# Attention maxima by 64 queries with two heads in a bank's partition halves, and scores by halves of 64 keys

## What is computed

```python
# 16 heads of 8; S = 512; causal
q_cos, q_sin, k_cos, k_sin = ...            # layer 0; layer 1 has plain q and k
scores = (einsum('bhqd,bhkd->bhqk', q_cos, k_cos) + einsum('bhqd,bhkd->bhqk', q_sin, k_sin)) / sqrt(8)
scores = where(tril(ones((S, S))), scores, -inf)
attn = softmax(scores, axis=-1)
out = einsum('bhqk,bhkd->bhqd', attn, v)    # then @ Wo.T, added to x
```

## Time and profile before

| | |
|---|---|
| median of 3 runs | 1248.75 us (1247.88 to 1258.58) |
| the profiled execution | 1242.17 us, span 1240.6 us |
| busy in the span | PE 982.9 us (79%), PE weight loads 648.0, DVE 831.4 (67%), ACT 678.7 (55%), POOL 639.1 (52%) |
| attention 0 | about 390 to 640 us of the span |
| attention 1 | about 970 to 1240 us |

### The profile page before, as it was taken

The page is one execution under the profiler, slowest core; times in us unless marked ns, Lnnn a source line. Parts: engine busy times, 40 slices in busy tenths (PEclk is TensorE's granted clock), DMA queues, the critical chain, the costliest instruction groups (busy, mean ns, idle before and its releaser), DMA issues. The chain is left out here.

```text
span 1240.6 us, 25928 instructions
## 1 busy us (share of the span) xinstructions
PE 982.9 (79%) x8908; PEld 648.0 (52%) x8908; DVE 831.4 (67%) x1829; ACT 678.7 (55%) x1293; POOL 639.1 (52%) x908
## 2 busy tenths in 40 slices
PE   2789663999883999999985563399999599999997
PEld 1456431777671455555543342388888345555553
DVE  1566341799995899999945776033333699999992
ACT  1356443777730677777763644122222277777775
POOL 3467637468774345455440666211110367777774
PEclk9899866899996799999997665699999599999999
DMA  4422032577796222222200333466664112112211
GB/s 134 114 50 54 27 115 72 140 208 211 212 155 126 68 71 71 70 77 77 74 8 26 101 107 109 133 191 189 183 194 145 43 47 54 54 53 54 56 47 29
DMA packets 151525, 122.57 MB, mean 99 GB/s; under 512 B 31712, under 2 KB 134032, under 8 KB 151408
## 3 DMA queue, kind: packets, MB, share of 16 engines
q1 hardware_dynamic: 141664, 102.89, 30.4%
q0 software_dynamic: 8016, 17.71, 4.8%
q10 hardware_dynamic: 1728, 0.46, 0.2%
HBM read 75.75 MB, written 42.61 MB: 95 GB/s over the span
## 5 line engine op out<-in xcount | busy, mean ns | idle before, releaser
L2117 ACT ACTIVATE attend_probs<-attend_attend_ps 128x512 f32<-128x512 f32 x640 | 350.8, 601 | 155.0 <-PE attend_attend_ps L2185 146.9
L2084 POOL TENSOR_SCALAR_AFFINE_SELECT attend_probs<-attend_probs 128x512 f32<-128x512 f32 x256 | 159.7, 636 | 189.8 <-ACT attend_probs L2117 189.3
L2185 PE MATMUL attend_attend_ps<-attend_q,attend_ks 50*128 50x512 f16 (+3 forms) x1024 | 235.2, 306 | 22.4 <-ACT attend_probs L2117 19.9
L2153 PE MATMUL attend_attend_ps<-attend_ks,attend_q 48*128 48x512 f16 (+3 forms) x1024 | 191.7, 317 | 32.4 <-DMA attend_ks<-k_stack 24.8
L2198 PE MATMUL attend_attend_ps<-attend_probs,attend_vals 128*32 128x512 f32 (+3 forms) x2048 | 182.3, 453 | 0.0
L2280 DVE TENSOR_REDUCE attend_neg_max<-attend_attend_ps 128x2 f32<-128x1024 f32 x128 | 155.0, 1211 | 10.0 <-PE attend_attend_ps L2165 10.0
L2165 PE MATMUL attend_attend_ps<-identb,stairs 64*128 64x128 bf16 (+1 forms) x1280 | 144.6, 213 | 0.0
L2185 PEld LDWEIGHTS attend_attend_ps<-attend_q,attend_ks 50*128 50x128 f16 x1024 | 71.3, 94 | 118.2 <-ACT attend_probs L2117 76.9
L2282 DVE TENSOR_REDUCE attend_neg_max<-attend_attend_ps 128x2 f32<-128x768 f32 x128 | 121.7, 951 | 9.7 <-PE attend_attend_ps L2165 8.2
L2165 PEld LDWEIGHTS attend_attend_ps<-identb,stairs 64*128 64x128 bf16 x1280 | 104.5, 100 | 18.1 <-issue 4.9
L1900 PE MATMUL experts_experts_ps<-experts_rowsT,experts_w_in 128*128 128x256 f32 (+1 forms) x468 | 110.8, 387 | 1.6 <-ACT experts_rowsT L1849 1.5
(11 more groups left out here) (317 smaller groups left out, 1988.3 us busy)
## 6 DMA issues: line engine op xcount, KB each, us to landing
experts_w_in<-in_L_ffn_w_dram SPq DMA_DIRECT2D x78, 176.0 KB, 2.4
q_stack<-middle_parts SPq DMA_DIRECT2D x24, 256.0 KB
k_stack<-middle_parts SPq DMA_DIRECT2D x24, 256.0 KB
attend_q<-q_stack SPq DMA_DIRECT2D x64, 96.0 KB
attend_ks<-k_stack SPq DMA_DIRECT2D x64, 96.0 KB
middle_w_in<-in_L_ffn_W_dram SPq DMA_DIRECT2D x23, 256.0 KB, 2.6
middle_w_out<-in_L_ffn_W_dram SPq DMA_DIRECT2D x23, 256.0 KB, 3.0
experts_rows<-sorted POOLq DMA_DIRECT2D x39, 128.0 KB, 2.5
```

Of the source, the lines that this page charges most:

```text
L2084: pool.affine_select(out=block_, in_=block_, compare_op=ALU.is_ge, fill=0.0, base=0, pattern=[[0, GH], [1, P]], channel_multiplier=-1).the ...
L2117: act.activation(probs[:, u.par, 2 * c + side, :], ps[:, PROB + side, :], ACT.Exp, scale=SCALE ** -2)\
L2153: pe.matmul(ps[:, bank + side, col:col + (qt + 1) * P], q[rows(side, KR), g, pair, qt * P:(qt + 1) * P], ks[rows(side, KR), g, pair, 0:(qt ...
L2185: mm = pe.matmul(ps[:, PROB + side, col:col + S - kt * P], ks[rows(side, KM), g, pair, kt * P:(kt + 1) * P], q[rows(side, KM), g, pair, kt ...
```

## The change

Maxima are taken by blocks of 64 queries (QS = 8 of them). In each of PE's products for the maxima the output is 64 partitions x up to 512 columns, and two heads share a bank, one in partitions 0 to 63 and one in 64 to 127; pair 0 and pair 1 have a bank each and opposite halves (`half`), so the four heads use the four quarters of the array. Chunks are now one or two blocks (`max_chunk`): 8 | 7 and 1 | 6 and 2 | 5 and 3 | 4 times 64 keys. The stairs are one matmul for each head and chunk, over both blocks. DVE reduces with one instruction for each block. The maxima of a unit lie by pair, part and block in the 32 partitions of `maxT` and by head in its columns, so four DMAs, each from 16 partitions x 64 columns, take them to `q`. The probabilities' products are cut in halves of 64 keys (outputs of 64 partitions), with the same banks, columns and order. ACT's, POOL's and the mix's work is as before.

```diff
+    H, QS = P // 2, 2 * QT
...
-        neg_max = sb("neg_max", [P, 2, 2, HP, QT])
-        max_parts = sb("max_parts", [P, 2, 2, 2, HP * QT], F16)
-        maxT = sb("maxT", [2 * GH * QT, 2, P], F16)
+        neg_max = sb("neg_max", [P, 2, HP, QS])
+        max_parts = sb("max_parts", [P, 2, HP, 2, QS], F16)
+        maxT = sb("maxT", [HP * 2 * QS, 2, P], F16)
...
-        max_in = [signal(f"max_in{i}", 2, 16) for i in range(2)]
+        max_in = [signal(f"max_in{i}", GH, 16) for i in range(2)]
...
         def max_chunk(c):
-            if c == 4:
-                return [(0, 1, 0), (1, 1, 256)]
-            return [(c // 2, 3, 0)] if c % 2 == 0 else [(c // 2, 2, 0), (c // 2, 0, 384)]
+            if c == 0:
+                return [(QS - 1, 0)]
+            return [(QS - 1 - c, 0), (c - 1, (QS - c) * H)] if c < 4 else [(3, 0)]
+
+        def half(side, pair):
+            first = H * ((side + pair) % 2)
+            return slice(first, first + H)
...
-                    for side in range(2):
-                        sp.dma_start(q[64 * side + KR:64 * side + KM, u.group, :, :], maxT[16 * side:16 * side + 16, u.par, :])\
-                          .then_inc(max_in[u.par].sem, 16)
+                    for pair in range(HP):
+                        for side in range(2):
+                            sp.dma_start(q[64 * side + KR:64 * side + KM, u.group, pair, :],
+                                         maxT[pair * 2 * QS:(pair + 1) * 2 * QS, u.par, half(side, pair)]).then_inc(max_in[u.par].sem, 16)
...
-                for n, (pair, qt, col) in enumerate(blocks):
-                    for side in range(2):
-                        pe.matmul(ps[:, bank + side, col:col + (qt + 1) * P], q[rows(side, KR), g, pair, qt * P:(qt + 1) * P],
-                                  ks[rows(side, KR), g, pair, 0:(qt + 1) * P], start=(n == 0), stop=False)
...
+                for n, (qs, col) in enumerate(blocks):
+                    for pair in range(HP):
+                        for side in range(2):
+                            pe.matmul(ps[half(side, pair), bank + pair, col:col + (qs + 1) * H],
+                                      q[rows(side, KR), g, pair, qs * H:(qs + 1) * H], ks[rows(side, KR), g, pair, 0:(qs + 1) * H],
+                                      start=(n == 0), stop=False)
+                diagonal = [col // H + qs for qs, col in blocks]
+                apart = diagonal[-1] - diagonal[0] if len(blocks) == 2 else 1
+                for pair in range(HP):
+                    for side in range(2):
+                        here = slice(64 * side, 64 * side + 64)
+                        span = ps[half(side, pair), bank + pair, :].rearrange("p (n t) -> p n t", t=H)
+                        mm = pe.matmul(span[:, diagonal[0]:diagonal[-1] + 1:apart, :], k.stairs[here, H + H * side:P + H * side],
+                                       k.identb[here, here].unsqueeze(1).broadcast_to([64, len(blocks), H]), start=False, stop=True)
+                    mm.then_inc(scored.sem, 1)
...
                 for pair, kt, col in prob_chunk(c):
-                    mm = pe.matmul(ps[:, PROB + side, col:col + S - kt * P], ks[rows(side, KM), g, pair, kt * P:(kt + 1) * P],
-                                   q[rows(side, KM), g, pair, kt * P:S], start=True, stop=True)
+                    for first in (0, H):
+                        mm = pe.matmul(ps[first:first + H, PROB + side, col:col + S - kt * P],
+                                       ks[rows(side, KM), g, pair, kt * P + first:kt * P + first + H], q[rows(side, KM), g, pair, kt * P:S],
+                                       start=True, stop=True)
...
+                for qs, col in max_chunk(c):
+                    ins = dve.tensor_reduce(neg_max[:, u.par, :, qs], pair_banks[:, :, col:col + (qs + 1) * H], X_AXIS, ALU.max, negate=True)
```

More of the change, by code:

```diff
@@ L2150, in maxima @@
                 blocks = max_chunk(c)
-                for n, (pair, qt, col) in enumerate(blocks):
-                    for side in range(2):
-                        pe.matmul(ps[:, bank + side, col:col + (qt + 1) * P], q[rows(side, KR), g, pair, qt * P:(qt + 1) * P],
-                                  ks[rows(side, KR), g, pair, 0:(qt + 1) * P], start=(n == 0), stop=False)
-                first = blocks[0][2] + blocks[0][1] * P
-                apart = blocks[1][2] + blocks[1][1] * P - first if len(blocks) == 2 else P
@@ L2158, in maxima @@
-                start = first // apart * apart
-                for half in range(2):
-                    for side in range(2):
-                        stair = P // 2 + P // 2 * side - P // 2 * half
-                        here = slice(64 * side, 64 * side + 64)
-                        span = ps[:, bank + side, start:start + apart * len(blocks)].rearrange("p (n t) -> p n t", t=apart)
-                        col = first - start + 64 * half
-                        mm = pe.matmul(span[:, :, col:col + 64], k.stairs[here, stair:stair + P],
-                                       k.identb[here, here].unsqueeze(1).broadcast_to([64, len(blocks), 64]),
-                                       start=False, stop=(half == 1))
-                        if half == 1:
-                            mm.then_inc(scored.sem, 1)
+                for n, (qs, col) in enumerate(blocks):
[4 more added lines that the diff above has]
+                                      start=(n == 0), stop=False)
@@ L2171, in turn_maxima @@
             def turn_maxima(u):
                 pe.wait_ge(parts_done.sem, parts_done.done(u))
-                pe.matmul(ps[0:2 * GH * QT, TURN, 0:P], max_parts[:, u.par, :, :, :].rearrange("p s a b -> p (s a b)"),
+                pe.matmul(ps[0:HP * 2 * QS, TURN, 0:P], max_parts[:, u.par, :, :, :].rearrange("p h a s -> p (h a s)"),
                           k.identh[:, :], start=True, stop=True)\
@@ L2179, in probabilities @@
                 if c == 0 and side == 0:
-                    pe.wait_ge(max_in[u.par].sem, (u.pair + 1) * 32)
+                    pe.wait_ge(max_in[u.par].sem, max_in[u.par].done(u.pair))
                 if u.past(1) or c >= 1:
@@ L2274, in reduce @@
                 pair_banks = ps[:, first:first + 2, :]
[L2275 to L2283 removed]
+                for qs, col in max_chunk(c):
+                    ins = dve.tensor_reduce(neg_max[:, u.par, :, qs], pair_banks[:, :, col:col + (qs + 1) * H], X_AXIS, ALU.max, negate=True)
                 ins.then_inc(maxed.sem, 1)
             def split_maxima(u):
[L2288 removed]
+                flat = neg_max[:, u.par, :, :]
                 parts = max_parts[:, u.par, :, :, :]
@@ L2300, in copy_maxima @@
                 if u.past(2):
-                    dve.wait_ge(max_in[u.par].sem, u.pair * 32)
-                dve.tensor_copy(maxT[:, u.par, :], ps[0:2 * GH * QT, TURN, 0:P])\
+                    dve.wait_ge(max_in[u.par].sem, max_in[u.par].done(u.pair - 1))
+                dve.tensor_copy(maxT[:, u.par, :], ps[0:HP * 2 * QS, TURN, 0:P])\
                    .then_inc(maxT_ready.sem, 1)
```

10 lines of the change are left out of this document (removed).

## The result

| | before | after |
|---|---|---|
| median | 1249.18 us (4 runs) | 1297.0 us (1285.65 to 1309.69, 4 runs) |
| profiled execution | 1242.17 us, span 1240.6 | 1289.64 us, span 1288.1 |
| attention 0, first to last CAST | 232.8 us | 244.6 us |
| attention 1, first to last CAST | 234.8 us | 264.5 us |

The ratio is 1.0336, 95% interval 1.022 to 1.0452: slower by some 3.4%. It leaves out the longest of the four executions after, 1309.69 us, which counts as a slow run (clock 0.87); the median takes in all four. (CAST is the copy of the turned maxima, L2302 before, L2306 after; its start is C. There are 32 in each attention.

The account below looks back on a forecast made before the run. DVE bounds the kernel, the maxima's way back 0.56 us behind; four issues make plain steps 7.96 us. Four steps gain +1.8 and +1.45, times 7.5, plus 5 for ends, less 2: +27 us, 1276 us, range 1228 to 1306.

Parts of the forecast that it names:

- the likeliest case: Whole kernel: four DMA issues delay PE's scores, plain step 7.96 against 7.23 us; 1276 us, by itself 1263 to 1290; chance 0.62.
- Rival E: PE, idle 2.1 us in each 8, loses its clock in some steps: +24 us, 1300 us; chance 0.04.
- What bounds the kernel: Plain step of 7.23 us: DVE runs almost without a hole; the maxima's way back has 0.56 us of slack.
- Four issues, 0.64 us apart: SP's queue behind each CAST: four maxima DMAs instead of two, 0.64 us from start to start, the last starting at C+2.22.
- Rival B: SP's four issues cost no more than two, so DVE's gain shows: plain step 6.68 us, 1217 us; chance 0.12.
- D: Gain and loss meet, with a DMA issue near 0.4 us: 1244 to 1260 us; chance 0.12.
- PE gets its maxima at C+2.22+2.21: PE's first scores: 2.21 us after the last issue starts at C+2.22, so C+4.43 instead of C+3.15.
- Row end 8.03: Step holding the end of a batch row: PE's shorter chunks 3 and 4 bring it to 8.03 us against 8.21.
- Reductions, -0.6 us: DVE's maxima reductions: 4608 elements in 8 instructions instead of 5120 in 7; DVE needs about 6.5 us a step.
- Quarters run all at once: PE's maxima matmuls: four array quarters overlap, about -0.3 us a step; wrong if chunk c=2 takes over 0.8 us to its mix.
- Gotcha 2 and the load price: PE weight loads: column tiling excludes the fast load; 84 loads 4.5 us, PE some 8.1 us if none hidden.
- Attention 1, "+1.45" for four steps: Attention 1: four steps, 30.45 us before, grow by 1.45 us, against +1.8 in attention 0.

Follow-up runs that it names:

- x9: The kernel after with attention 1's gathers left out except for the first 128 rows, which are joined to every row: 1262.22 us, ratio 1.0127.
- x1: The kernel before with four maxima DMAs instead of two, and none of the 64-row parts: 1263.04 us, ratio 1.0185.
- x4: The kernel after with two maxima DMAs instead of four, the maxima turned with three matmuls: 1243.05 us, ratio 1.0008.
- x6: The kernel after with the second of attention 1's two gathers a unit, and its join, left out: 1278.84 us, ratio 1.0226.
- x8: x4 with DVE's subtraction that forms the low parts moved behind the c=0 reduction: 1272.51 us, ratio 1.0207.
- x3: The kernel after with the probabilities' products whole again (128 keys), four DMAs and quartered maxima kept: 1467.03 us, ratio 1.1813.
- x2: The kernel before with only the probabilities' products cut in halves of 64 keys: 1369 to 1501 us in four runs.

## Why the prediction came out as it did

The sign holds, and the mechanism of the likeliest case for about half of the loss. The size was 21 us short (1276 against 1297.0). In the profiled executions +47.5 us stand against +27: attention 0 has 11.8 where about 15 were forecast, attention 1 29.7 for 12, and 6.0 lie outside the stretches from first to last CAST. The longer way through SP explains most of attention 0 and at most 9.1 us of attention 1; 20.6 us there have another cause. The likeliest case by itself was 1263 to 1290, and the kernel lies above it. The range reached further for the sake of rivals, of which only E happened, and in small, so that it holds 1297.0 is in part luck. (Without the gathers, x9, the ratio of 1.0127 would be 1265 us, inside the likeliest case.)

- **What bounds the kernel:** DVE bounds it, and PE's first scores have 0.56 us to spare behind it; that held. But the maxima's DMAs have more. The forecast took the 2.21 us from the last issue to PE for the DMA's own way, though the row at 594.07 ends its wait with ACT. By the semaphore events the last of the maxima land at 593.60 = C+2.68, 1.74 us behind the last issue, and PE is held on until 594.04 by the exponential that ends at 593.93. (The weight load ahead of that row names the DMA, as the only semaphore of its own.) The waits of PE in 480 to 640, before and after:

```profile
PE attend_attend_ps L2185 <- ACT attend_probs L2117: 7.1, 16, 0.6
```

```profile
PE attend_attend_ps L2195 <- DMA attend_q<-attend_maxT: 16.5, 13, 1.4
```

  So the last issue could start not 0.56 but about 1.0 us later without loss. It starts 1.33 later, and x1, which adds nothing but the two issues, pays the difference: 7.53 for 7.23 us.
- **Four issues, 0.64 us apart:** held (2.59 us for four; median 611 ns over 256). Rival B is out, D too. (The 2.85 us that rival B set the two issues against hold ACT's wait too; to the landing it is 2.38.)
- **"PE gets its maxima at C+2.22+2.21":** mis-sized. The last issue starts at 593.55 + 2.59 - 0.62 = 595.52 and PE at 597.26, 1.74 us later, not 2.21; the maxima land 1.67 us behind that start (median). This is the term of the sum that was mis-sized in attention 0, for the reason above. In x4, with two DMAs, PE comes 2.55 us behind the last issue (587.98, scores at 590.53), but the maxima have landed at 589.74, and it is ACT again that ends the wait. So the plain step is 7.58 and not 7.96, and PE idle 1.21 us where 1.5 to 2.1 were named.
- **Row end 8.03:** it is 8.43 (before 8.21). I let the shorter chunks 3 and 4 bring add_row forward by 0.2 us; it starts at C+4.65 (613.02 - 608.37), 0.14 later than before. This takes back, for each row, what the plain steps had been overpriced by: for attention 0 the two errors, and the four steps of 8.1 to 8.4 us at a lower clock (x1, which has none there, has 241.2 for 244.6), leave 11.8 us where about 15 were forecast.
- **Reductions, -0.6 us:** -0.39. By form, in the groups of the trace, the eight of a unit mean 0.28, 0.41, 0.55, 0.69, 0.83, 0.94, 1.08 and 1.22 us, 6.00 in sum; the seven of before 1.23, 2 x 1.21, 2 x 0.95 and 2 x 0.42, 6.39. I priced the further instruction at 0.1; the forms lie on a line of 1.05 ns an element and 0.15 us each. The subtraction gave back another 0.44 where it met the mask. So DVE's need is about 7.1 us a step (7.07 - 0.39 + 0.44), not 6.5, and x4 bears it out: with the DMA term gone, 7.32 and no hole. DVE busy in four steps stays at 28.20, where about 26 was named. For the same reason DVE waits 0.26 us before the c=0 reduction in the profile after, where I had named 1.5 as the sign. I called the split "the same shapes" and priced it so; its neighbour on POOL had changed. Rival B's 1217 us was thus never to be had.
- **Quarters run all at once:** held; from the scores to the mix of chunk 2 it is 0.63 us (592.64 to 593.27); the bound of 0.8 that I had named isn't reached. Gotcha 2 and the load price, which the Trainium skill has in "TensorEngine Tiling (Array Packing)" and "TensorE: Matmul & The Clock Gate", LDWEIGHTS, don't bite here: with 84 loads a unit PE still waits 1.21 us. (The 8.1 us that the prediction set beside them can't be worked out from figures that it shows.)
- **Attention 1, "+1.45" for four steps:** failed. It was carried over from attention 0, and its term for POOL's gathers was nothing, without a reason given. x9 shows that with the gathers away it would be 243.9 - 234.8 = 9.1 us for the attention; with them it is 29.7. The missing term is 264.5 - 243.9 = 20.6 us. It isn't the clock: four steps at full clock take 33.9 us against x9's 31.1. That this is nearly the error of the forecast is chance: -3 in attention 0, -3 in the rest of attention 1 and +6 outside the two cancel.
- **Rival E:** it came true in small. The clock is at 1.00 in most steps, but it fell in the four places above, which cost 2.8 us in attention 0 and some 2 in attention 1, where 24 us were priced; x6, in which PE's waits are uneven, has eleven such places. Over the whole it is 0.885 against 0.895 before.

What stays open: why PE's releases come late beside a gather in some kernels and not in others. x4 and x8 differ in the place of one DVE instruction, and PE's matmuls lie nearly alike against the gathers; x4 has none of over 0.44 us in attention 1, x8 has some of 1.3 us and more in nearly each step. Before has one place of over a microsecond, x1 five.

## What to carry to other kernels

Count what a layout does to the way back, not only to the work: two more tiny DMAs on one queue, which put the last issue back by 1.3 us where 1.0 was to spare, cost 0.3 us a step, and a dearer turn on PE that keeps two DMAs (x4) costs nothing that shows. The time from an issue to the engine that waits is the DMA's only if the DMA ended that wait: look which release came last before you price a longer way by it. A gain on an engine counts only up to the next loop behind it, and where several loops stand within a few tenths of a microsecond, price each instruction with its neighbours on the other engines as they will then lie. Two stages that run the same code beside different background work need two forecasts.

## What the runs showed of the hardware

- Beside an indirect gather of POOL (0.95 to 0.99 us of issue), releases of PE can come late: mostly 1.25 to 1.7 us behind the gather's start and up to 1.9 us behind the matmul's modelled end, while PE goes on starting matmuls. The gathers cost 20.6 us in the kernel after and 25.2 us in x8 (259.4 - 234.2), and nothing in x4. It shows in a profile as idle time "<-PE" behind matmuls that were long done.
- The DVE subtraction with two inputs in SBUF ends with POOL's mask where that began just before it: 0.61 against 0.175 us.
- Matmuls that cut the array in 64 rows x 64 columns and in 64 x 128 didn't overlap; mixing them took 0.41 us more in the chunk that was read (x3), and in both kernels that mixed them (x2, x3) the granted clock stood at 0.50 for long stretches.
- The granted clock fell for short stretches in kernels whose PE waits longest: none behind the first steps of an attention before and in x4 (PE idle 0.43 and 0.62 us ahead of the first scores), four in the kernel after (1.21 us). The two in attention 0 cost 1.4 us each. No run tests the waits as the cause.
- One issue of a small mismatched DMA takes 0.61 us on SP's queue whether it carries 2 or 4 KB (medians 611 and 617 ns), and its data has landed 1.67 or 1.74 us behind the start of the issue.
